# A mixture-of-experts kernel whose last layer norm moves from a pass of its own into the expert loop

## The chip, the cores and the metric

The kernel runs on one core of a Trainium2 chip. The metric is the device time of one execution in microseconds (us), the median of several. The core has five engines that run side by side: TensorE (PE in the profile, with its weight loads as PEld), VectorE (DVE), ScalarE (ACT), GpSimd (POOL) and SyncE (SP), and 16 DMA engines that move data between HBM and the on-chip memory.

## The reference, cut to what matters

```
x  = layernorm(x + attention(x))            # 16 batches x 1024 tokens x 256 values, float32
# mixture of experts: 8 experts, hidden size 1024, two experts per token
logits = x @ wr.T ; vals, idx = top_k(logits, 2) ; gates = softmax of the two
pos  = running count of tokens per expert ; keep = pos < 5120       # a slot beyond 5120 is dropped
h    = gelu(x[slot] @ w1[e] + b1[e]) ; y = (h @ w2[e] + b2[e]) * gate
out  = layernorm(x + sum over the token's kept experts of y)
```

A token has at most two expert entries, in two different experts, and one or both may be dropped.

## The kernel before, in words

T is 16384 tokens, a tile has 128 partitions. The program has three phases, each a block in which the five engines run their own instruction streams and wait for each other by semaphores; between blocks all engines meet.

Phase A goes through the 16 batches, two per loop turn. It computes attention and the first layer norm. All engines' streams are written out by hand in a pipelined order: while TensorE works on batch b, ScalarE and VectorE finish the layer norm and the router of batch b-1. The normalised rows x1 (tile `x1_sb`, two of them, used in turn) are stored by SyncE to two HBM buffers, `x1_rows` and `sum_rows` (`acc_dram`). ScalarE's body is in this order: four copies `kt_out`, parts of the next batch's softmax, `gate_exp`, the copy `g_hi` (L432), `normalize` half 0 (L368), more softmax, `m_hi`, `qt`, `normalize` half 1. TensorE's `maps()` needs `g_lo`, which VectorE makes from `g_hi` (L621). For each token VectorE computes the table slots of its two entries, and GpSimd scatters 16 small DMAs per batch (L323) that write (token, gate) into `slot_table`; entries with no token hold the number of a padding row.

Phase B goes through the experts in order, and within one through blocks of 256 slots, 129 blocks in all. Block n on each engine:

- GpSimd (`body`): waits for the transposes of block n's rows (`xt_ready`), `gather(n+1)`: copies the row numbers (L972) and starts two indirect DMAs that fetch 256 rows of x1 into `rows` (L975); then `put(n)`: two small copies of index and gate (L983, L984), a wait for `y_done`, and two indirect DMAs that add `y` into `sum_rows` in HBM (L988). What `put(n)` writes is the result of the block before n.
- TensorE: `up(0) up(1) up(2) down(0) up(3)`, then `transpose_rows(n+1)` (L1110, waits for `gathered`), `down(1) down(2) down(3)`. Each up and down is 12 matmuls. `down(g)` waits for `h_lo(g)`.
- ScalarE: gelu and the copy `h_hi` (L1031, L1034) for g = 0 to 3, then `split_hi(n+1)` of the transposed rows (L1022).
- VectorE: `h_lo(g)` (L1066) for g = 0 to 3; after g = 1 `scale_y` (L1055), the product of the previous block's result and its gate; after g = 3 `split_lo` (L1047); last `y_raw` = `y_ps` + bias (L1082). In the first two blocks of an expert it also splits the next expert's weights in 8 pieces, one behind each `h_lo` (a cast, L1076, and a subtraction, L1078).
- SyncE loads the weights of expert e+2 when those of e+1 have been split.

Phase C (L1163 on) reads `sum_rows` batch by batch into a ring of four tiles, takes mean and variance on VectorE (L1208, L1211), the reciprocal root on GpSimd (L1223 to L1229, the power at L1225), normalises on ScalarE (L1239), and SyncE stores `out`.

```
def body(n, e, eu):                    # GpSimd, phase B, before
    pool.wait_ge(xt_ready, n + 1)
    gather(n + 1)
    put(n)
```

Of the kernel before, what the change touches and what calls it, by code (L numbers as in the profile page):

```python
# [6 lines left out]
def build(nc, x, x_t, wq, wk, wv_t, wo, wo_t, bo, bo_t, wr_t, w1, b1_t, w2, b2, out):  # L7
# [9 lines left out]
    P = 128  # L17
# [21 lines left out]
    acc_dram = nc.dram_tensor("sum_rows", (T + BLK, D), F, kind="Internal").ap()  # L39
    table_dram = nc.dram_tensor("slot_table", (SLOTS, 2), I, kind="Internal").ap()  # L40
    x1_store = x1_dram[0:T, :].rearrange("(b p t) d -> b p (t d)", p=P, t=TILES)
    acc_store = acc_dram[0:T, :].rearrange("(b p t) d -> b p (t d)", p=P, t=TILES)
# [4 lines left out]
    with outer:  # L47
# [38 lines left out]
        with ExitStack() as phase:  # L86
# [36 lines left out]
            rstd, nshift = sb("rstd", [P, TILES]), sb("nshift", [P, TILES])  # L123
            minus_half = sb("minus_half", [P, TILES])
# [22 lines left out]
            entry = [sb(f"entry{i}", [P, 2, TILES, 2], I) for i in range(2)]  # L147
            blocks_f = sb("blocks_f", [P, 2 * E + 1])
            counts = sb("counts", [P, E])
            pad_entries = sb("pad_entries", [P, TCOLS, 2], I)  # L150
# [44 lines left out]
            entries_written = sems("entries_written", 2)  # L195
            const_step = sem("const_step")
# [17 lines left out]
            def _(sp):  # L214
# [27 lines left out]
                for rows_dram in (x1_dram, acc_dram):  # L242
                    for t in range(BT):
                        sp.dma_start(rows_dram[T + t * P:T + (t + 1) * P, :], zero_rows[:, :]).then_inc(pads_stored, 16)
# [3 lines left out]
                load_xt(3)  # L248

                def body(pair, u, x_left=True, xt_left=True):  # L250
                    b = pair * 2 + u
                    if x_left:
                        sp.wait_ge(r_done, (b + 1) * TILES)
                        load_x(b + 2, u)
                    if xt_left:
# [3 lines left out]
                    for rows in (x1_store, acc_store):  # L259
                        sp.dma_start(rows[b].rearrange("p (t d) -> p t d", d=D), x1_sb[u][:, :, 0:D]).then_inc(x1_stored[u], 16)  # L260

                with sp.Fori(0, NB // 2 - 2) as pair:
                    for u in range(2):
                        body(pair, u)
# [4 lines left out]

                for u in range(2):  # L270
                    sp.wait_ge(x1_stored[u], 32 * (NB // 2))
                sp.wait_ge(pads_stored, 16 * (1 + 2 * BT))
# [3 lines left out]
            def _(pool):  # L276
# [28 lines left out]
                nc.gpsimd.iota(pad_entries[:, :, 0].rearrange("p (a t) -> p a t", t=BT), pattern=[[0, TCOLS // BT], [P, BT]], base=T, channel_multiplier=1).then_inc(pads_made, 1)  # L305
# [12 lines left out]

                def scatter(b, u):
# [8 lines left out]
                pool.wait_ge(pads_stored, 16 * (1 + 2 * BT))  # L328

                def body(pair, u, first, last):  # L330
                    b = pair * 2 + u
                    if not first:
                        norm_chain(b - 1)
                        scatter(b - 1, 1 - u)

                batches(pool, body)
                norm_chain(NB - 1)
                scatter(NB - 1, 1)
# [4 lines left out]
            def _(act):  # L343
# [20 lines left out]
                def normalize(b, u, half):  # L364
# [5 lines left out]
                    if half:  # L370
                        ins.then_inc(x1_done, 1)

# [19 lines left out]
                def body(pair, u, first, last):  # L392
# [60 lines left out]
                batches(act, body)  # L453
                gate_exp(NB - 1)
                for half in range(2):
                    normalize(NB - 1, 1, half)

# [3 lines left out]
            def _(dve):  # L461
# [55 lines left out]
                ROUTE_STEPS = 23  # L517

                def router(b, u, state):
# [37 lines left out]
                    def address(pair, scattered):  # L557
# [6 lines left out]
                                             ALU.arith_shift_right))  # L564
                        if scattered:
                            dve.wait_ge(entries_written[u], 16 * 2 * TILES * pair)
                            V.tensor_scalar(entry[u][:, :, :, 0], entry[u][:, :, :, 0], 2 * N, None, ALU.add)
                        V.scalar_tensor_tensor(where[u][:, :, :], slot_p[:, :, :], float(TCOLS), slot_c[:, :, :], ALU.mult, ALU.add)

                    def gates():  # L570
                        gate = entry[u][:, :, :, 1].bitcast(F)
# [13 lines left out]
                def statistics(b, u):  # L585
                    for t in range(TILES):
                        V.bn_stats(stats[:, t, :], x1_sb[u][:, t, 0:D]).then_inc(stats_done, 1)
                    wait_apart(dve, stats_done, TILES * (b + 1))
# [688 lines left out]
```

## Time and profile before

| | us |
|---|---|
| median of 3 runs | 2361.29 |
| lowest, highest | 2356.31, 2366.18 |
| profiled execution, its own time | 2358.53 |
| its span, first to last instruction | 2356.6 |
| PE busy / ACT / DVE / POOL | 2049.0 / 1136.2 / 1113.5 / 1111.8 |
| mean granted TensorE clock | 0.934 |

The page of the profile has the busy time of each engine, and the same in 40 slices of the span. Slices 14 to 38 of PE are nearly all nines: that is phase B. Before it PE is at 6 to 8 tenths (phase A), and in the last two slices PE does nothing while the DMA rate is highest (phase C). An engine's idle time is put down to the instruction that released it ("<-DVE y L1055"). A POOL span can begin before the engine is free: where a row of POOL starts inside the one before it, the true time is counted from that one's end.

### The profile page before, as it was taken

What the parts mean: (1) busy time and instruction counts of PE and PEld (TensorE: products, weight loads), DVE (VectorE), ACT (ScalarE), POOL (GpSimd) and SP (SyncE); (2) the same over time, 40 slices, a digit from 0 to 9 for tenths busy, and PEclk for the clock granted to TensorE, in tenths of its full rate; (3) what the DMA queues carried; (4) which work ended last, traced back from release to release, by engine and by line L of the source; (5) the groups of instructions that cost most, each with busy time, mean ns of one, the idle gap of its engine ahead of it and who ended that gap; (6) DMA issues with size and microseconds to landing.
All of it is one profiled execution on the core that took longest, in us unless ns stands there. A gap on an engine that the chain in (4) does not pass through costs nothing. (4 is left out here: it accounts for less than half of the span.)

```text
span 2356.6 us, 48196 instructions
## 1 busy us (share of the span) xinstructions
PE 2049.0 (87%) x16208; PEld 1987.8 (84%) x16209; DVE 1113.5 (47%) x2614; ACT 1136.2 (48%) x2516; POOL 1111.8 (47%) x1333
## 2 busy tenths in 40 slices
PE   7887887878744999999999999999999999999910
PEld 6776786777644999999999999999999999999910
DVE  3665565655563435345335333534543534333345
ACT  3444443434332555555555455455455555555547
POOL 0335454453544445444455444544544545444434
PEclk9998898989876999999999999999999999999965
DMA  4323233242223323222322322322322222222258
GB/s 165 108 73 124 90 103 111 72 143 71 68 81 95 80 46 81 45 45 45 79 47 49 76 45 47 80 45 45 80 45 45 45 45 46 46 46 46 46 204 377
DMA packets 130733, 190.10 MB, mean 81 GB/s; under 512 B 19088, under 2 KB 111760, under 8 KB 126480
## 3 DMA queue, kind: packets, MB, share of 16 engines
q0 software_dynamic: 58256, 68.60, 18.1%
q1 hardware_dynamic: 72448, 121.16, 14.8%
q8 instruction: 12, 0.20, 0.0%
q14 instruction: 17, 0.14, 0.0%
HBM read 104.05 MB, written 85.66 MB: 81 GB/s over the span
## 5 line engine op out<-in xcount | busy, mean ns | idle before, releaser
L1031 ACT ACTIVATE h_ps<-h_ps,b_sb 128x256 f32<-128x256 f32 x1032 | 418.5, 444 | 712.6 <-PE h_ps L1129 667.7
L988 POOL DMA_INDIRECT sum_rows<-y,put_idx x260 | 418.9, 1611 | 601.6 <-DVE y L1055 556.3
L1066 DVE TENSOR_TENSOR h_lo<-h_ps,h_hi 128x512 fp32r<-128x512 f32 x516 | 356.6, 691 | 628.7 <-ACT h_hi L1034 600.5
L1145 PE MATMUL y_ps<-w_hi,h_hi 128*128 128x256 f32 x2064 | 586.1, 284 | 0.0
L1129 PE MATMUL h_ps<-bt_hi,w_hi 128*128 128x256 f32 x2064 | 576.1, 279 | 3.2 <-issue 1.7
L1145 PE MATMUL y_ps<-w_hi,h_lo 128*128 128x256 f32 x2064 | 575.8, 279 | 0.0
L1145 PE MATMUL y_ps<-w_lo,h_hi 128*128 128x256 f32 x2064 | 575.1, 279 | 0.0
L1129 PE MATMUL h_ps<-bt_lo,w_hi 128*128 128x256 f32 x2064 | 574.0, 278 | 0.0
L1129 PE MATMUL h_ps<-bt_hi,w_lo 128*128 128x256 f32 x2064 | 574.0, 278 | 0.0
L323 POOL DMA_INDIRECT slot_table<-entry,where x256 | 277.8, 1085 | 304.2 <-DVE entry L575 228.7
L1129 PEld LDWEIGHTS h_ps<-bt_hi,w_hi 128*128 128x128 f32 x2064 | 389.6, 189 | 5.0 <-issue 3.2
L1145 PEld LDWEIGHTS y_ps<-w_hi,h_lo 128*128 128x128 f32 x2064 | 389.6, 189 | 0.0
L1129 PEld LDWEIGHTS h_ps<-bt_lo,w_hi 128*128 128x128 f32 x2064 | 388.7, 188 | 0.0
L1129 PEld LDWEIGHTS h_ps<-bt_hi,w_lo 128*128 128x128 f32 x2064 | 388.6, 188 | 0.0
L1145 PEld LDWEIGHTS y_ps<-w_hi,h_hi 128*128 128x128 f32 x2064 | 388.3, 188 | 0.0
L1145 PEld LDWEIGHTS y_ps<-w_lo,h_hi 128*128 128x128 f32 x2064 | 386.9, 187 | 0.0
L975 POOL DMA_INDIRECT rows<-x_rows,pick_idx x260 | 258.7, 995 | 159.6 <-POOL pick_idx L972 107.5
L1034 ACT ACTIVATE h_hi<-h_ps 128x512 fp32r<-128x512 f32 x516 | 309.0, 599 | 16.4
L788 PE MATMUL g_ps<-kt,x_raw 128*128 128x256 f32 x512 | 144.1, 437 | 85.1 <-issue 64.9
L788 PEld LDWEIGHTS g_ps<-kt,x_raw 128*128 128x128 f32 x512 | 108.9, 221 | 104.7 <-issue 78.7
L1082 DVE TENSOR_TENSOR y_raw<-y_ps,b_sb 128x512 f32<-128x512 f32 x129 | 89.3, 692 | 225.6 <-PE y_ps L1145 222.7
L403 ACT ACTIVATE kt<-t_ps 128x512 f32<-128x512 f32 x64 | 37.9, 598 | 185.4 <-remote 100.5
(191 smaller groups left out, 2843.9 us busy)
## 6 DMA issues: line engine op xcount, KB each, us to landing
xt_raw<-in_x_t SPq DMA_DIRECT2D x16, 1024.0 KB
x_raw<-in_x SPq DMA_DIRECT2D x16, 1024.0 KB
w_raw<-in_w SPq DMA_DIRECT2D x16, 1024.0 KB
x_rows<-x_sb SPq DMA_DIRECT2D x16, 1024.0 KB
sum_rows<-x_sb SPq DMA_DIRECT2D x16, 1024.0 KB
s_in<-sum_rows SPq DMA_DIRECT2D x16, 1024.0 KB, 8.9
out<-s_out SPq DMA_DIRECT2D x16, 1024.0 KB, 6.8
rows<-x_rows,pick_idx POOLq DMA_INDIRECT x260
```

The lines of the kernel that those rows point to most:

```text
L323: pool.indirect_dma_start(out=table_dram, out_offset=bass.IndirectOffsetOnAxis(ap=where[u][:, c, t:t + 1], axis=0), in_=entry[u][:, c, t, ...
L403: nc.scalar.activation(kt[:, j % 2, :], t_ps[:, j % 2, :], ACT.Copy).then_inc(kt_done, 1)
L788: ins = nc.tensor.matmul(g_sum[:, k, :], x_raw[u][:, t, k * P:(k + 1) * P], kt[:, j % 2, i * D:(i + 1) * D], start=(t == 0 and k == 0), st ...
L975: pool.indirect_dma_start(out=rows[:, t, :], out_offset=None, in_=x1_dram, in_offset=bass.IndirectOffsetOnAxis(ap=pick_idx[:, t:t + 1], ax ...
L988: pool.indirect_dma_start(out=acc_dram, out_offset=bass.IndirectOffsetOnAxis(ap=put_idx[:, t:t + 1], axis=0), in_=y[:, t, :], in_offset=No ...
L1031: nc.scalar.activation(half, half, ACT.Gelu_apprx_tanh, bias=b1_sb[:, bass.ds(e * FT + 2 * g + i, 1)]).then_inc(gelu_done, 1)
L1034: nc.scalar.activation(h_hi[:, g, :], h_ps[:, g, :], ACT.Copy).then_inc(h_hi_done, 1)
L1066: V.tensor_tensor(h_lo[:, g, :], h_ps[:, g, :], h_hi[:, g, :].bitcast(F), ALU.subtract).then_inc(h_lo_done, 1)
L1082: V.tensor_tensor(y_raw[:, :, :], y_ps[:, :, :], b2_sb[:, bass.ds(e * D, D)].rearrange("p (a d) -> p a d", a=1).broadcast_to([P, BT, D]), ...
L1129: ins = nc.tensor.matmul(h_ps[:, g, (f % 2) * BLK:(f % 2 + 1) * BLK], w[:, c:c + P], v[:, k, :], start=(i == 0), stop=(i == 3 * DK - 1))
L1145: ins = nc.tensor.matmul(y_ps[:, t, :], v[:, g, h:h + P], w[:, c:c + D], start=(f == 0 and t == 0 and part == 0), stop=(f == FT - 1 and t ...
```

## The change

Phase C and the buffer `sum_rows` are gone. A table entry has four words in place of two: token, place of the sum so far, gate, and a flag. The entry that lies in the higher slot is the token's last one if the other one isn't dropped; its second word is then the token, that of the first entry is out of range. Results go straight to `out` with plain indirect DMAs that skip rows out of range.

In phase B the first entry of a token writes x1 + gate * y, un-normalised, to `out`; the last one fetches that row as its `base`, adds gate * y, and normalises with the flag deciding by arithmetic (factor 1 and mean 0 where it isn't the last). x1 of a block stays on chip: ScalarE copies `rows` to `x1_next`, VectorE copies that to `base`, and `take_up_sums` overwrites by DMA those rows of `base` that have a sum in `out`. A token both of whose entries are dropped gets its result in phase A: ScalarE normalises x1 once more (`renormalize`, 8 activations per batch), and SyncE stores it to `out` where it stored the second copy of x1 before.

An expert has 5 blocks at least, where it had 4. The weights' split is spread over blocks 0, 2 and 3 of an expert. The first block of an expert on GpSimd (`first_body`) puts, waits until it has landed, and only then takes up sums; VectorE adds up late in the block after it (`turn == 1`).

```diff
@@ GpSimd, phase A @@
+                def norm_again(b, u):
+                    if not (isinstance(b, int) and b < 2):
+                        pool.wait_ge(alone_done, b - 1)
+                    nc.gpsimd.tensor_tensor(again[u][:, :], mean_var[:, :, 1], rstd[:, :], ALU.mult).then_inc(again_step, 1)
+                    nc.gpsimd.tensor_tensor(again[u][:, :], again[u][:, :], rstd[:, :], ALU.mult).then_inc(again_step, 1)
+                    nc.gpsimd.tensor_scalar(again[u][:, :], again[u][:, :], EPS, None, ALU.add).then_inc(again_step, 1)
+                    nc.gpsimd.tensor_tensor(again[u][:, :], again[u][:, :], minus_half[:, :], ALU.pow).then_inc(again_done, 1)
...
@@ ScalarE, phase A @@
+                def renormalize(b, u):
+                    act.wait_ge(again_done, b + 1)
+                    act.wait_ge(alone_stored, 16 * b)
+                    for t in range(TILES):
+                        ins = nc.scalar.activation(alone[:, t, :], x1_sb[u][:, t, 0:D], ACT.Copy, scale=again[u][:, t:t + 1])
...
                     if more:
                         q_softmax(b + 1, 1 - u, 1)
+                    if not first and not (isinstance(b, int) and b == 1):
+                        renormalize(b - 2, u)
                     if not first:
                         gate_exp(b - 1)
@@ VectorE, phase A, address() @@
+                        V.tensor_tensor(leads[:, 0, :], slot_i[:, 1, :], slot_i[:, 0, :], ALU.is_ge)
+                        step(V.tensor_tensor(leads[:, 1, :], slot_i[:, 0, :], slot_i[:, 1, :], ALU.is_ge))
...
+                        V.scalar_tensor_tensor(entry[u][:, :, :, 1], leads[:, :, :], DROPPED, entry[u][:, :, :, 0], ALU.mult, ALU.add)
+                        for c in range(2):
+                            V.scalar_tensor_tensor(entry[u][:, c, :, 3].bitcast(F), slot_f[:, 1 - c, :], DROPPED, leads[:, c, :],
+                                                   ALU.is_ge, ALU.is_ge)
@@ GpSimd, phase B @@
+                def root(n):
+                    pool.wait_ge(var_done, n + 1)
+                    G.tensor_tensor(rstd[:, :], rstd[:, :], minus_half[:, :], ALU.pow).then_inc(root_done, 1)
+
+                def take_up_sums(n):
+                    pool.wait_ge(base_done, n + 1)
+                    G.tensor_copy(base_idx[:, :], column(n + 1, 1)).then_inc(base_ready, 1)
+                    wait_apart(pool, base_ready, n + 1)
+                    for t in range(BT):
+                        pool.indirect_dma_start(
+                            out=base[:, t, :], out_offset=None, in_=out_dram,
+                            in_offset=bass.IndirectOffsetOnAxis(ap=base_idx[:, t:t + 1], axis=0),
+                            bounds_check=T - 1, oob_is_err=False).then_inc(base_loaded, 16)
+
+                def scalars(n):
+                    G.tensor_copy(put_gate[:, :], column(n, 2).bitcast(F))
+                    G.tensor_copy(put_last[:, :], column(n, 3).bitcast(F)).then_inc(last_ready, 1)
+                    wait_apart(pool, last_ready, n + 1)
+                    G.tensor_scalar(put_part[:, :], put_last[:, :], -1.0, 1.0, ALU.mult, ALU.add).then_inc(put_ready, 1)
+
+                def put(n, more=True):
+                    pool.wait_ge(put_done, 16 * BT * n + 16)
+                    G.tensor_copy(put_idx[:, :], column(n, 0)).then_inc(put_idx_ready, 1)
+                    pool.wait_ge(y_done, n + 1)
+                    if more:
+                        scalars(n + 1)
+                    wait_apart(pool, put_idx_ready, n + 1)
                     for t in range(BT):
                         pool.indirect_dma_start(
-                            out=acc_dram, ..., in_=y[:, t, :], in_offset=None, compute_op=ALU.add).then_inc(added, 16)
+                            out=out_dram, ..., in_=y[:, t, :], in_offset=None,
+                            bounds_check=T - 1, oob_is_err=False).then_inc(put_done, 16)
...
+                def first_body(n, e, eu):
+                    pool.wait_ge(next_done, n + 1)
+                    gather(n + 1)
+                    root(n)
+                    put(n)
+                    pool.wait_ge(put_done, 16 * BT * (n + 1) + 16)
+                    take_up_sums(n)
+
                 def body(n, e, eu):
-                    pool.wait_ge(xt_ready, n + 1)
+                    pool.wait_ge(next_done, n + 1)
                     gather(n + 1)
+                    take_up_sums(n)
+                    root(n)
                     put(n)
@@ ScalarE, phase B, behind split_hi(n + 1) @@
+                def keep_rows(n):
+                    act.wait_ge(base_done, n)
+                    act.wait_ge(gathered, 16 * BT * (n + 1))
+                    nc.scalar.activation(x1_next[:, :, :], rows[:, :, :], ACT.Copy).then_inc(next_done, 1)
@@ VectorE, phase B @@
+                def add_up(n):        # waits y_raw_done, put_ready, base_loaded
+                    for t in range(BT):
+                        ins = V.scalar_tensor_tensor(y_raw[:, t, :], y_raw[:, t, :], put_gate[:, t:t + 1], base[:, t, :],
+                                                     ALU.mult, ALU.add)
+                def next_base(n):     # waits next_done
+                    V.tensor_copy(base[:, :, :], x1_next[:, :, :]).then_inc(base_done, 1)
+                def spread(n):        # bn_stats and bn_aggr of 2 tiles, then
+                    V.tensor_scalar(rstd[:, :], mean_var[:, :, 1], EPS, None, ALU.add).then_inc(var_done, 1)
+                    V.tensor_tensor(mean[:, :], mean_var[:, :, 0], put_last[:, :], ALU.mult).then_inc(sum_step, 1)
+                def factors(n):
+                    dve.wait_ge(root_done, n + 1)
+                    V.tensor_tensor(rstd[:, :], rstd[:, :], put_last[:, :], ALU.mult).then_inc(sum_step, 1)
+                    V.tensor_tensor(rstd[:, :], rstd[:, :], put_part[:, :], ALU.add).then_inc(sum_step, 1)
+                def finish_rows(n):   # waits put_done
+                    for t in range(BT):
+                        ins = V.tensor_scalar(y[:, t, :], y_raw[:, t, :], mean[:, t:t + 1], rstd[:, t:t + 1], ALU.subtract, ALU.mult)
+
+                    late = turn == 1
+                    if not late:
+                        add_up(n)
+                        next_base(n)
                     for g in range(UNITS):
                         h_lo(g)
-                        if g == 1:
-                            scale_y(n)
+                        if late and g == 1:
+                            add_up(n)
+                            next_base(n)
+                        if g == (2 if late else 0):
+                            spread(n)
+                        if g == (3 if late else 1):
+                            factors(n)
+                            finish_rows(n)
                         if g == UNITS - 1:
                             split_lo(n + 1)
-        (all of phase C)
```

## Rows read from the trace of the kernel before

**Rows 1.** Busy time by stage: us, busy (count) of each engine, clock, DMA share.

```profile
740.00:2250.00 1510.00, 1496.81 (x12901) 1493.92 (x12900) 650.42 (x1147) 773.85 (x1678) 744.42 (x907) 1.00 0.30 53
2262.00:2356.60 94.60, 0.00 (x0) 0.00 (x0) 53.31 (x256) 64.29 (x128) 37.84 (x65) 0.50 0.86 355
```

**Rows 2.** Costliest groups of the page: count, busy us, mean ns, idle before.

```profile
L988 POOL DMA_INDIRECT sum_rows<-y,put_idx x260 | 418.9, 1611 | 601.6 <-DVE y L1055 556.3
L1082 DVE TENSOR_TENSOR y_raw<-y_ps,b_sb 128x512 f32<-128x512 f32 x129 | 89.3, 692 | 225.6 <-PE y_ps L1145 222.7
```

**Rows 3.** POOL in order of time, one block of phase B: start us, us.

```profile
1534.21 1.61 POOL L988 DMA_INDIRECT sum_rows<-y,put_idx  x1 [4.79 <-DVE y L1055]
1536.13 1.58 POOL L988 DMA_INDIRECT sum_rows<-y,put_idx  x1 [0.30 <-issue]
1537.14 0.77 POOL L972 COPY pick_idx<-table 128x2 int32 x1
1538.78 1.01 POOL L975 DMA_INDIRECT rows<-x_rows,pick_idx  x1 [0.87 <-POOL pick_idx L972]
1540.09 0.98 POOL L975 DMA_INDIRECT rows<-x_rows,pick_idx  x1 [0.30 <-DMA sum_rows<-y,put_idx]
...
1541.21 0.18 POOL L984 COPY put_gate<-table 128x2 f32 x1
```

**Rows 4.** DVE in order of time over the same block.

```profile
1530.76 0.69 DVE L1066 TENSOR_TENSOR h_lo<-h_ps,h_hi 128x512 fp32r<-128x512 f32 x1 [2.20 <-ACT h_hi L1034]
...
1532.73 0.61 DVE L1055 TENSOR_SCALAR y<-y_raw,put_gate 128x256 f32<-128x256 f32 x2
...
1539.47 0.69 DVE L1082 TENSOR_TENSOR y_raw<-y_ps,b_sb 128x512 f32<-128x512 f32 x1 [1.87 <-PE y_ps L1145]
...
1551.00 0.69 DVE L1082 TENSOR_TENSOR y_raw<-y_ps,b_sb 128x512 f32<-128x512 f32 x1 [1.74 <-PE y_ps L1145]
```

**Rows 5.** PE in order of time, transposes: at an expert's start, and inside an expert.

```profile
1522.95 0.66 PE L1110 MATMUL tb_ps<-ident,rows 128*128 128x128 f32 x4 [0.73 <-DMA rows<-x_rows,pick_idx]
...
1534.47 0.60 PE L1110 MATMUL tb_ps<-ident,rows 128*128 128x128 f32 x4
```

**Rows 6.** POOL in order of time, end of phase B and phase C.

```profile
2248.61 0.18 POOL L983 COPY put_idx<-table 128x2 int32 x1 [2.52 <-DMA sum_rows<-y,put_idx]
...
2271.82 1.67 POOL L1225 TENSOR_TENSOR rstd_c<-rstd_c,minus_half_c 128x8 f32<-128x8 f32 x1
...
2273.97 0.25 POOL L1229 TENSOR_SCALAR nshift_c<-nshift_c 128x8 f32<-128x8 f32 x1 [0.19 <-POOL nshift_c L1227]
```

**Rows 7.** DVE in order of time, the last block of phase B.

```profile
2247.79 0.69 DVE L1082 TENSOR_TENSOR y_raw<-y_ps,b_sb 128x512 f32<-128x512 f32 x1 [1.87 <-PE y_ps L1145]
```

**Rows 8.** Groups by line, phase C.

```profile
L1208 DVE BATCH_NORM_STATS2 stats_c<-s_in 128x6 f32<-128x256 f32 x128 | 43.3, 411 | 40.0 <-DMA s_in<-sum_rows 40.0
```

**Rows 9.** Groups by line, 1000 to 2200 us.

```profile
L1076 DVE CAST w_hi<-w_raw 128x512 fp32r<-128x512 f32 x40 | 19.5, 487 | 0.0
```

**Rows 10.** DVE in order of time, phase A.

```profile
502.28 0.17 DVE L562 TENSOR_SCALAR slot_p<-slot_i 128x16 int32<-128x16 int32 x1
...
504.89 0.48 DVE L633 SCALAR_TENSOR_TENSOR m_raw<-o_ps,rzk,bo_sb 128x264 f32<-128x264 f32 x1
...
510.68 2.28 DVE L480 TENSOR_TENSOR w_lo<-xt_raw,w_hi 128x2048 fp32r<-128x2048 f32 x1
```

**Rows 11.** ACT in order of time, phase A.

```profile
497.87 0.21 ACT L375 ACTIVATE gap_exp<-gap 128x8 f32<-128x8 f32 x1 [0.67 <-DVE gap L546]
499.07 0.60 ACT L432 ACTIVATE g_hi<-g_ps 128x512 fp32r<-128x512 f32 x1 [1.00 <-PE g_ps L788]
499.57 2.07 ACT L368 ACTIVATE x_sb<-x_sb,nshift,rstd 128x256 f32<-128x256 f32 x4
```

**Rows 12.** POOL in order of time, phase A.

```profile
510.71 3.09 POOL L323 DMA_INDIRECT slot_table<-entry,where  x1 [0.30 <-issue]
```

**Rows 13.** PE in order of time, phase A, first matmul of `maps()`.

```profile
502.73 0.28 PE L710 MATMUL g_ps<-wvo_hi,g_hi 128*128 128x264 f32 x1
```

More of the change, by code:

```diff
@@ L123, in build @@
             rstd, nshift = sb("rstd", [P, TILES]), sb("nshift", [P, TILES])
+            again = [sb(f"again{i}", [P, TILES]) for i in range(2)]
+            alone = sb("alone", [P, TILES, D])
             minus_half = sb("minus_half", [P, TILES])
@@ L254, in body @@
                         load_x(b + 2, u)
+                    if not (isinstance(pair, int) and pair == 0 and u == 0):
+                        store_alone(b - 1)
                     if xt_left:
@@ L258, in body @@
                     sp.wait_ge(x1_done, b + 1)
-                    for rows in (x1_store, acc_store):
-                        sp.dma_start(rows[b].rearrange("p (t d) -> p t d", d=D), x1_sb[u][:, :, 0:D]).then_inc(x1_stored[u], 16)
-                with sp.Fori(0, NB // 2 - 2) as pair:
+                    sp.dma_start(x1_store[b].rearrange("p (t d) -> p t d", d=D), x1_sb[u][:, :, 0:D]).then_inc(x1_stored[u], 16)
+                for u in range(2):
+                    body(0, u)
+                with sp.Fori(1, NB // 2 - 2) as pair:
                     for u in range(2):
@@ L304, in _ @@
                 made(nc.gpsimd.memset(pad_entries[:, :, :], 0))
-                nc.gpsimd.iota(pad_entries[:, :, 0].rearrange("p (a t) -> p a t", t=BT), pattern=[[0, TCOLS // BT], [P, BT]], base=T, channel_multiplier=1).then_inc(pads_made, 1)
+                for w in range(2):
+                    made(nc.gpsimd.iota(pad_entries[:, :, w].rearrange("p (a t) -> p a t", t=BT), pattern=[[0, TCOLS // BT], [P, BT]], base=T, channel_multiplier=1))
+                nc.gpsimd.memset(leads[:, :, :], 0).then_inc(pads_made, 1)
                 def norm_chain(b):
@@ L942, in experts @@
                         blocks, before = blocks_of(eng, half * 2 + eu)
-                        with eng.Fori(0, blocks) as block:
+                        if first_body is not None:
+                            first_body(before, half * 2 + eu, eu)
+                        with eng.Fori(0 if first_body is None else 1, blocks) as block:
                             body(before + block, half * 2 + eu, eu)
@@ L1009, in body @@
                     put(n)
-                experts(pool, body)
+                experts(pool, body, first_body=first_body)
                 total = all_blocks(pool)
-                put(total)
-                pool.wait_ge(added, 16 * BT * (total + 1) + 16)
+                root(total)
+                put(total, False)
+                pool.wait_ge(put_done, 16 * BT * (total + 1) + 16)
                 pool.wait_ge(gathered, 16 * BT * (total + 1))
@@ L1088, in expert @@
                     blocks, before = blocks_of(dve, e)
-                    for turn in range(2):
-                        body(before + turn, e, eu, None if last else turn)
-                    with dve.Fori(2, blocks) as block:
+                    for turn in range(4):
+                        body(before + turn, e, eu, turn, not last)
+                    with dve.Fori(4, blocks) as block:
                         body(before + block, e, eu)
```

234 lines of the change are left out of this document (107 added, 127 removed).

## Prediction, made before the changed kernel ran

> **What bounds the kernel now.** I read the stages first, then the order of time inside one block of phase B on each engine, then the end of the kernel and one batch of phase A. In phase B PE is busy 1496.8 of 1510 us at a granted clock of 1.00, the full 2.4 GHz [rows 1]: TensorE bounds 64% of the kernel. One block takes 11.55 us there (the 11.53 between two `y_raw` starts in [rows 4]; neighbours have 11.59), and there are 129 [rows 2]. Every other engine has idle time that costs nothing: POOL waited 556 us in all for `y` before its puts, 4.3 us per block [rows 2]. Phase C is another kind of stage: PE does nothing and the DMA engines are 86% busy [rows 1]. So the change takes away a stage that moves data and puts its arithmetic beside a stage that PE fills. The question is whether it stays beside it.
>
> **Removed: phase C.** The last `y_raw` ends at 2247.79 + 0.69 = 2248.5 [rows 7], the span at 2356.6: 108.1 us come after it. The new tail behind that `y_raw`: two additions 0.9, statistics and variance 1.3, the power 0.6, factors and final rows 1.05 (prices below), 0.87 before an indirect DMA, two puts 2.3, 2.5 for the landing (a wait of POOL for a put lasted 2.52 behind its issue [rows 6]), and 0.5 to close: 10. Saved: 98 us. This is sure; the reads and adds in HBM in phase B that go with it save nothing, since no row has PE waiting for them.
>
> **Phase B, POOL's round.** In the new order POOL's work per block is a closed ring: `y_done` -> scalars -> puts -> gather(n+1) -> sums(n) -> root(n) -> VectorE's factors and final rows -> `y_done`. POOL can't begin root(n) before both transfers are issued, and VectorE can't finish `y` before root. So a block can't be shorter than the sum, however early rows are ready:
> - scalars: two copies 0.31 (from 1541.07 to 1541.39), 0.04 to start, then a self-wait 0.19 and a small operation 0.25 [rows 3, 6]. An indirect DMA behind a wait starts 0.87 late, after a copy as after `y` (1533.34 to 1534.21) [rows 3, 4]; that lies partly beside the small operation. 1.2 to 1.7, I take 1.45.
> - puts: before, 1.61 + 0.30 + 1.58. Those accumulate; the plain gather takes 1.01 + 0.30 + 0.98 = 2.29 [rows 3]. I take 2.29, since the new put is plain; the bound above is 3.49.
> - gather: copy 0.19, 0.87, 2.29: 3.35 [rows 3]. Sums: the same kinds of instruction, 3.35.
> - root: the power over 128x8 takes 1.67, a small operation 0.25 [rows 6]. If it goes by element, 2 columns of 8 take 0.25 + 1.42 / 4 = 0.6; bounds 0.25 and 1.67. I take 0.6.
> - VectorE: two dependent small operations of 0.2 (0.17 each [rows 10] and the gap), two products 0.61 [rows 4], 0.04 to start: 1.05.
>
> Sum 12.1 us against 11.55. POOL's idle 4.3 is used up: it gave 1.2 back by the plain puts, and took 3.35 + 0.6 + 0.9 + the turn-around through VectorE. Bounds: 11.5 with every lower end, 14.6 with every upper one.
>
> VectorE itself fits: it had 2.20 idle before `h_lo(0)` [rows 4], and two additions of 0.48 [rows 10] and a copy of about 0.42 to 0.49 [rows 9] go there; statistics are 0.41 per tile [rows 8]. ScalarE's extra copy, 0.6, is hidden by its idle time. But while VectorE waits for root in `factors` at g = 1, `h_lo(2)` stands behind it, and `down(2)` on PE behind that. Count from the start of `h_lo(0)`: transposes at 3.70 (1534.47 - 1530.77 [rows 4, 5]), `down(1)` at 4.1, and 1.4 per down (12 of 96 matmuls) gives 5.5 for `down(2)`. The new `y_done` is naturally at 3.9, `h_lo(2)` 0.65 later, so PE has 0.9 of slack once, and from then on each block takes 12.1. An expert has 16 blocks on average; in blocks 4 to 15: 12 x 0.55 - 0.9 = 5.7 us; 8 experts: 46 us.
>
> **Phase B, the start of an expert.** In block 0 root comes early, `y_done` at 3.8. Then puts issued at 3.8 + 3.74 = 7.5, landed (2.5) at 10.05, sums issued 13.4, and only then gather for block 2, issued 16.75, landed 19.25. PE wants these rows at 11.55 + 3.70 = 15.25: it stalls 4.0. Rows landed sooner would make this 3.3. Block 1: base landed at 15.9, additions and copy to 17.2, sums to 20.55, root 21.15, `y_done` 22.2. One ring later, at 34.3, comes the `y_done` of block 2; a weight piece stands behind it (a cast 0.49 [rows 9] and a subtraction as long as `h_lo`, together 1.2 us), then `h_lo(2)`, which ends at 36.15. PE, whose block began its count at 23.1 + 4.0 = 27.1, wants it at 32.6: 3.5, and 0.4 more for `h_lo(3)`. Block 3 is free again (sums are issued before its statistics). Pieces in block 0: 0.6. Together 8.5 per expert. Today's stalls there go off: phase B is 1510 us for 129 blocks, 19 more than 129 x 11.56 [rows 1, 2], 2.3 per expert, of which the wait for rows beside the weights' load, 0.73 [rows 5], stays; 1.5 goes. 7 x 8 = 56 us. Phase B: +102.
>
> **Phase A.** `renormalize` is 8 activations, as long as the four that take 2.07 [rows 11]: 4.0 us at ScalarE, put before `g_hi`. It had 0.67 idle before `gap_exp` and 1.00 before `g_hi` at 499.07 [rows 11]; `g_hi` now begins 4.0 - 1.7 = 2.3 later, at 501.4. Behind it: `g_lo`, `maps()` on PE, which began at 502.73 [rows 13] and so keeps its place to within 0.2; but VectorE's slot arithmetic comes after `g_lo` and is 0.5 longer (five small operations at 0.1 and one step more at 0.2), so the next maximum, `m_raw`, `m_hi` and `m_lo` come 1.5 later, and `attend(0)` with them. 14 batches x 1.5: +22 us; bounds 0 (the delay is caught up in the 4 us of idle between batches) and 50. `norm_again` on POOL (2.7 us per batch) is hidden by its 16 us of waiting for the router; the store to `out` replaces another of the same size, and stands in SyncE's queue between loads whose own waits end later, so nothing waits for it. Set-up on POOL and the minimum of 5 blocks: nothing, no expert has fewer.
>
> **Sum.** 2358.5 (the profiled execution's own time) - 98 + 102 + 22 = 2384.5. The median is 2.8 above the profiled execution, so 2387.
>
> **A rule weighed.** A scatter of POOL took 3.09 us, not the 1.0 of a gather [rows 3], when VectorE began a 2.28 us operation with two operands in on-chip memory 0.03 before it [rows 10, 12]. Base additions and copy are such operations, and fall beside the gather's second DMA. The Trainium skill ("SBUF — State Buffer", on the shared port pair) says that the pair is an exclusive lock held for the whole instruction, taken by a float32 copy, which enters a 2-port mode, and for reads by an operation with two inputs there. The trace agrees for two inputs, 2.28 beside 3.09. By that rule the ring grows by up to the copy's 0.42, which is the fourth case below.
>
> **Cases.**
> - Forecast, 0.42: ring of 11.9 to 12.5; 2360 to 2420. A third of it lies under 2375.
> - Ring within 11.55, 0.30. All lower ends: the 0.87 hides, power 0.25. PE stays the bound in plain blocks, the starts of experts cost 5 x 8 = 40, phase A 5: 2358.5 - 98 + 45 = 2305 (to 2345 with ring 11.7). For it: the two waits of 0.87 before gather and sums are idle time, not work. Against it: they are in every block. This is the other side; it decides at a ring of 11.7.
> - The put or the power stays at its upper price, 0.08: ring 13.2, 12 x 1.65 - 0.9 = 19 per expert, 9 at the start: 224, 2358.5 - 98 + 224 + 22 = 2507. Against it: the plain gather at 0.98.
> - VectorE and POOL block each other, 0.13: ring 12.5, 40 us more: 2424.
> - Phase A costs the 50: 0.07, 2412.
>
> That the change doesn't do what it says is not among them: phase C can't be left in. The range is 2315 to 2450, which leaves about 0.1 below and 0.1 above; the forecast's own is 2360 to 2420. A measurement here tells 0.5%, 12 us, from no change: faster 0.26 (the second case but its top), same 0.18 (a third of the first and that top), slower 0.56.
>
> **What would show it.** In the new trace, groups of POOL by line: puts at 1.0 rather than 1.6, the power 0.6. `y_raw` start to start: 12.1 in blocks 4 to 15; POOL's longest wait no longer `y` but under 1.2 per block; VectorE idle before the first factor product "<-POOL rstd" about 0.6; PE idle 0.5 per block before an L1145 matmul, and in each expert one stall of 3 to 4 us before L1110 "<-DMA rows". Phase A: `maps()` at the same distance from the batch's start, `attend(0)` 1.5 later. The forecast is wrong if PE stays over 98% busy in phase B.

## The result: slower by 5.2%, 95 us above the forecast

The changed kernel takes 2482.03 us (median of 4, 2480.21 to 2486.15), the kernel before 2360.71 beside it: ratio 1.0515, 95% interval 1.0493 to 1.0537. The profiled execution took 2480.21, its span 2478.5. I had 2387, range 2315 to 2450: right in sign, outside in size. By stage, from the `y_raw` starts of the two traces (profiled executions, us):

| | before | after | change | forecast |
|---|---|---|---|---|
| start to first `y_raw` | 755.8 | 760.6 | +4.8 | +22 |
| first to last `y_raw` (phase B) | 1492.0 | 1706.6 | +214.6 | +102 |
| of it: 97 blocks from the fifth of an expert on | 11.56 each | 13.03 each (median 12.84) | +143 | +46 |
| of it: first four blocks of 8 experts | | | +72 | +56 |
| behind the last `y_raw` start | 108.8 | 11.2 | -97.5 | -98 |

The stage row, where [rows 1] had PE busy 1496.81 of 1510 us:

```profile
740.00:2470.00 1730.00, 1598.38 (x12904) 1568.85 (x12904) 1025.05 (x2568) 855.87 (x1808) 1036.45 (x1685) 0.98 0.17 56
```

There are as many matmuls as before (12904, before 12901), but PE is idle for 132 us of this stretch, where it was for 13, and the granted clock is 0.98 in the mean. The groups of the page after (answering to [rows 2]): the puts fell from 1611 to 1045 ns, and PE now has 96 us of idle time ahead of the second layer:

```profile
L1083 POOL DMA_INDIRECT out<-y,put_idx x260 | 271.8, 1045 | 130.1 <-issue 128.1
L1048 POOL DMA_INDIRECT rows<-x_rows,pick_idx x260 | 266.1, 1023 | 156.1 <-issue 113.7
L1062 POOL DMA_INDIRECT base<-out,base_idx x258 | 263.9, 1023 | 159.7 <-issue 82.0
L1317 PE MATMUL y_ps<-w_hi,h_hi 128*128 128x256 f32 x2064 | 615.3, 298 | 96.4 <-DVE h_lo L1227 96.0
```

POOL after in order of time, one plain block, from the first put to the next (answers to [rows 3]); between two rows stands idle time, in brackets with its releaser:

```profile
1117.26 1.10 POOL L1083 DMA_INDIRECT out<-y,put_idx  x1 [0.69 <-issue]
1118.67 0.99 POOL L1083 DMA_INDIRECT out<-y,put_idx  x1 [0.31 <-issue]
1119.64 0.22 POOL L1045 COPY pick_idx<-table 128x2 int32 x1
1120.74 1.09 POOL L1048 DMA_INDIRECT rows<-x_rows,pick_idx  x1 [0.88 <-issue]
1122.13 0.97 POOL L1048 DMA_INDIRECT rows<-x_rows,pick_idx  x1 [0.30 <-DVE base L1185]
1123.10 0.20 POOL L1059 COPY base_idx<-table 128x2 int32 x1
1124.18 1.04 POOL L1062 DMA_INDIRECT base<-out,base_idx  x1 [0.88 <-issue]
1125.53 1.00 POOL L1062 DMA_INDIRECT base<-out,base_idx  x1 [0.31 <-issue]
1126.56 0.74 POOL L1054 TENSOR_TENSOR rstd_b<-rstd_b,minus_half_b 128x2 f32<-128x2 f32 x1
1127.26 0.18 POOL L1077 COPY put_idx<-table 128x2 int32 x1
1128.72 0.18 POOL L1069 COPY put_gate<-table 128x2 f32 x1 [1.28 <-DVE y L1211]
...
1130.10 1.10 POOL L1083 DMA_INDIRECT out<-y,put_idx  x1 [0.69 <-issue]
```

From put to put 12.84 us, and POOL's only long wait for another engine is the 1.28 for `y`. VectorE after, over the same block (answers to [rows 4]), shows why that wait is no slack: VectorE itself waited 2.09 for the power, and gave `y` back 1.25 behind it. The ring is closed.

```profile
1114.97 0.74 DVE L1211 TENSOR_SCALAR y<-y_raw,mean_b,rstd_b 128x256 f32<-128x256 f32 x2
...
1121.39 0.69 DVE L1185 COPY base<-x_next 128x512 f32<-128x512 f32 x1
...
1127.33 0.16 DVE L1203 TENSOR_TENSOR rstd_b<-rstd_b,put_last 128x2 f32<-128x2 f32 x1 [2.09 <-POOL rstd_b L1054]
1127.52 0.16 DVE L1205 TENSOR_TENSOR rstd_b<-rstd_b,put_part 128x2 f32<-128x2 f32 x1
1127.81 0.74 DVE L1211 TENSOR_SCALAR y<-y_raw,mean_b,rstd_b 128x256 f32<-128x256 f32 x2
1128.46 1.28 DVE L1227 TENSOR_TENSOR h_lo<-h_ps,h_hi 128x512 fp32r<-128x512 f32 x2
```

The end after, DVE in order of time (answers to [rows 7]); the span ends 11.2 behind the start of this row:

```profile
2467.21 0.69 DVE L1250 TENSOR_TENSOR y_raw<-y_ps,b_sb 128x512 f32<-128x512 f32 x1 [3.64 <-PE y_ps L1317]
```

### The profile page after: what moved, and what is told of

It is laid out like the page before. It is cut to its first block, busy times and chain, and to the rows that moved or that the text cites. A ratio compares the mean times of both kernels' runs of the same rounds, so it can differ in the third digit from the quotient of the medians.

```text
span 2478.5 us, 52379 instructions
## 1 busy us (share of the span) xinstructions
PE 2146.0 (87%) x16208; PEld 2059.5 (83%) x16209; DVE 1444.7 (58%) x3868; ACT 1199.0 (48%) x2646; POOL 1404.7 (57%) x2114
## 4 chain that ended last, share of the span: by engine, by line
POOL 19%; issue 17%; PE 16%; DVE 14%; DMA 2%; POOLq 2%; DVEq 1%; ACT 0%; ACTq 0%
PE y_ps L1317 14%; POOL base L1062 7%; POOL rows L1048 5%; POOL rstd_b L1054 4%; DVE y_raw L1250 2%; DVE base L1185 2%; DVE h_lo L1227 2%; DVE y L1211 2%; PE h_ps L1301 2%; DVE y_raw L1178 2%; POOL out L1083 1%; DMA rows<-x_rows,pick_idx 1%; POOL base_idx L1059 1%; DVE rstd_b L1205 1%; DVE rstd_b L1203 1%
## 5 line engine op out<-in xcount | busy, mean ns | idle before, releaser
L1317 PE MATMUL y_ps<-w_hi,h_hi 128*128 128x256 f32 x2064 | 615.3, 298 | 96.4 <-DVE h_lo L1227 96.0
L1317 PE MATMUL y_ps<-w_lo,h_hi 128*128 128x256 f32 x2064 | 592.1, 287 | 0.0
L1317 PE MATMUL y_ps<-w_hi,h_lo 128*128 128x256 f32 x2064 | 591.7, 287 | 0.0
L1301 PE MATMUL h_ps<-bt_lo,w_hi 128*128 128x256 f32 x2064 | 584.7, 283 | 0.0
L1317 PEld LDWEIGHTS y_ps<-w_hi,h_hi 128*128 128x128 f32 x2064 | 401.8, 195 | 119.2 <-DVE h_lo L1227 118.7
L1227 DVE TENSOR_TENSOR h_lo<-h_ps,h_hi 128x512 fp32r<-128x512 f32 x516 | 346.0, 685 | 98.5 <-ACT h_hi L1151 87.8
L1317 PEld LDWEIGHTS y_ps<-w_hi,h_lo 128*128 128x128 f32 x2064 | 402.2, 195 | 0.0
L1317 PEld LDWEIGHTS y_ps<-w_lo,h_hi 128*128 128x128 f32 x2064 | 401.9, 195 | 0.0
L1062 POOL DMA_INDIRECT base<-out,base_idx x258 | 263.9, 1023 | 159.7 <-issue 82.0
L1083 POOL DMA_INDIRECT out<-y,put_idx x260 | 271.8, 1045 | 130.1 <-issue 128.1
```

The lines of the kernel that those rows point to most:

```text
L1062: pool.indirect_dma_start(out=base[:, t, :], out_offset=None, in_=out_dram, in_offset=bass.IndirectOffsetOnAxis(ap=base_idx[:, t:t + 1], a ...
L1083: pool.indirect_dma_start(out=out_dram, out_offset=bass.IndirectOffsetOnAxis(ap=put_idx[:, t:t + 1], axis=0), in_=y[:, t, :], in_offset=No ...
L1227: V.tensor_tensor(h_lo[:, g, :], h_ps[:, g, :], h_hi[:, g, :].bitcast(F), ALU.subtract).then_inc(h_lo_done, 1)
L1301: ins = nc.tensor.matmul(h_ps[:, g, (f % 2) * BLK:(f % 2 + 1) * BLK], w[:, c:c + P], v[:, k, :], start=(i == 0), stop=(i == 3 * DK - 1))
L1317: ins = nc.tensor.matmul(y_ps[:, t, :], v[:, g, h:h + P], w[:, c:c + D], start=(f == 0 and t == 0 and part == 0), stop=(f == FT - 1 and t ...
```

## The experiments

Theory 1: POOL's closed ring sets each plain block. Rivals: the landing of puts at an expert's start, VectorE and POOL lengthening each other, PE or VectorE by themselves, phase A. "After" is the changed kernel, "before" the one before it. Runs of one group shared a chip and the runs of the kernel before on it; ratios are against those. "Plain block" is the median distance of two `y_raw` starts from an expert's fifth block on: 11.55 us before, 12.84 after. Before: 2362.83 in the first group.

**Root first.** `root(n)` ahead of `take_up_sums(n)` in the loop body:

```
-    take_up_sums(n)
     root(n)
+    take_up_sums(n)
```

> One edit to the changed kernel: in GpSimd's plain body of phase B root(n) stands before take_up_sums(n) and not behind it; no engine does more or less. Theory 1 (the closed round y_done - scalars - puts - gather - sums - root - VectorE - y_done sets the block, 12.84 us in the trace of after): VectorE's 1.27 us and the 0.17 behind it then run beside the sums, POOL's own work is left, 11.4 to 11.8 us; PE needs 11.56. Plain blocks 11.6 to 11.8, starts of experts unchanged, time about 2370 (2355 to 2390). Rival A (VectorE has too much work: 3.5 us more per block, and h_lo queues behind it) and rival B (the DMA engines or the shared memory ports slow everything): the work is the same, so 12.8 per block and 2482 stay.

2373.2 us, ratio 1.0048 (1.0025 to 1.0071). One swap of two calls takes the ratio from 1.0515 to 1.0048, some 110 of the 121 us. Plain block 11.94. By the traces phase B is 115 us shorter: 81 in the plain blocks, and 34 in the first four blocks of the experts, where none was expected. The ring theory holds for the plain blocks; but PE had next to no idle time in them (0.08 us per block) and yet took 11.94, not 11.55, which no theory had. That led to the place runs below.

**Early index.** The copies of the gather's and the sums' indices a block earlier:

```
 def put(n):
     copy put_idx
+    copy pick_idx for gather(n + 2)
     wait y_done, scalars(n + 1)
+    copy base_idx for sums(n + 1)
```

> The changed kernel with its order, but the copies of the gather's and the sums' row numbers are made one block earlier, beside GpSimd's wait for y, into the same tiles (a tile of its own for the first block of an expert), so that the indirect DMAs don't start 0.88 behind a copy of 0.2. Theory 1: the round loses about 2 x (0.2 + 0.88 - 0.3) = 1.55 and gets back about 0.2: 11.5, so PE's 11.56 sets plain blocks again; time 2340 (2325 to 2365). If the 0.88 is work of GpSimd that only moves: 12.4 to 12.8 and 2440 or more. Rivals A and B: no change.

2411.4, ratio 1.0211 (1.0187 to 1.0235): half of the gain that I had expected. Plain block 12.39. POOL got to the power earlier, but VectorE, in order of time in this kernel, couldn't use it yet: `h_lo(1)` stands ahead of the factors in its program, and ScalarE gave the input of `h_lo(1)` only at 1108.11:

```profile
1108.11 0.69 DVE L1242 TENSOR_TENSOR h_lo<-h_ps,h_hi 128x512 fp32r<-128x512 f32 x1 [1.64 <-ACT h_hi L1166]
1108.72 0.15 DVE L1218 TENSOR_TENSOR rstd_b<-rstd_b,put_last 128x2 f32<-128x2 f32 x1
```

The power had ended at 1107.67. So the ring got a new member, ScalarE's `h_hi(1)`. (The tiles that this edit adds also moved the matmuls' operands; their pace was 0.116 us here, see the place runs. PE had idle time in these blocks, 0.43 us each, so it isn't what set them.)

**First sums free.** In an expert's first block the sums come from `x1_rows`, without the wait for landed puts (the sums are then not the right ones):

```
-    pool.wait_ge(put_done, 16 * BT * (n + 1) + 16)
-    take_up_sums(n)
+    take_up_sums(n, x1_dram)
```

> The changed kernel, but in the first block of an expert the sums are fetched from x1_rows and not from out, and the wait for the landed put before it is gone (the values of those rows are another's; the DMA is of the same size and skips the same rows). Theory 1 for the starts (put, its landing, sums and only then the gather for block 2 stand in one row on GpSimd): the wait of 2 to 2.5 us goes, block 2 of an expert falls from 17.2 to about 15, 8 x 2 to 3 us: time 2460 (2452 to 2468). If the starts are set by VectorE's late order and its weight pieces instead: unchanged within 4 us.

2480.4, ratio 1.0506 (1.0480 to 1.0532): no gain that can be told. In the mean over the experts, block 1 fell from 13.72 to 12.41 us, and block 2 rose from 17.23 to 18.04, block 3 from 12.32 to 12.61. Most of what the wait had cost, PE then waited later.

**More on POOL, before.** The kernel before with one more copy and one more pair of gathers per block:

```
     gather(n + 1)
+    copy more_idx; two indirect gathers into more_rows
     put(n)
```

> The kernel before with one more copy of row numbers and one more pair of indirect DMAs per block on GpSimd (256 rows of x1 into a tile that nothing reads), put between gather and put. It adds 3.4 us to POOL per block and as many bytes as a full take-up of sums, but no turn-around. Theory 1: POOL had 4.3 us of idle per block, 0.9 stays, PE stays the bound: within 0.5% of before (2361), at most 2375 where POOL's rare pauses of 2 us now show. Rival B (DMA engines or ports): 5% slower, as the changed kernel is.

2423.3, ratio 1.0268 (1.0240 to 1.0295): a miss. POOL in order of time in this run:

```profile
1412.51 0.18 POOL L994 COPY put_gate<-table 128x2 f32 x1
1414.31 1.62 POOL L998 DMA_INDIRECT sum_rows<-y,put_idx  x1 [1.61 <-DVE y L1069]
...
1424.55 0.17 POOL L994 COPY put_gate<-table 128x2 f32 x1
1426.33 1.62 POOL L998 DMA_INDIRECT sum_rows<-y,put_idx  x1 [1.61 <-DVE y L1069]
```

The old kernel has such a ring too: VectorE's `y` waits for `put_gate`, copied behind the gathers, and POOL for `y`. The 1.61 are 0.62 of VectorE and 0.87 in front of an indirect DMA, not slack. The ring here is 12.02 from put to put; without the 3.2 added it is 8.8, so the slack before was 11.55 - 8.8 = 2.7 us, not the 4.3 that the wait showed. From put to put it takes 11.98 to 12.08 in 103 of 128 blocks and more in the others (12.7 where an expert starts), 1555 us in all, where phase B is 1553: the ring set this kernel's phase B. The plain block, 11.89 by the median, is shorter because PE, behind after an expert's start, then makes up for it. The edit also moved the matmuls' operands by 32 bytes, and their pace from 0.116 to 0.118 us; no put came later by that.

**Place of the tiles.** An unused tile stands ahead of `rows`; its size moves `rows` and every tile allocated behind it. Second group (before 2358.37): the changed kernel, and root-first, with a larger one, and the kernel before without it.

```
 after, root first:  - sb("spare", [P, 16])   + sb("spare", [P, 32])
 before:             - sb("spare", [P, 16])
```

> The changed kernel with 64 bytes more of unused tile ahead of rows, nothing else. In the kernel before, rows, bt_hi, bt_lo, h_hi and h_lo begin 64 bytes above a multiple of 128 in each partition; the new small tiles moved them to a multiple of 128, and matmuls now start 0.119 us apart where they started 0.1156 us apart, at the same granted clock. Two theories. Place: the distance is set by where those tiles lie; here it goes back to 0.1156, but a plain block stays at 12.84, since there POOL's ring and not PE sets it; only the starts of experts gain, about 10 us: 2470 (2462 to 2480). Traffic: the distance is set by what POOL, VectorE and the DMAs do beside PE; here it stays 0.119 and the time 2482.

2487.3, ratio 1.0559 (1.0518 to 1.0600). Matmuls are 0.116 apart again, plain block 12.80: POOL's ring sets it, and PE only waits longer (for `h_lo` 121 us in phase B, where it was 96). The 10 us at the starts didn't come.

> The kernel before without its unused tile spare of 64 bytes, so that rows, bt_hi, bt_lo, h_hi and h_lo begin at a multiple of 128 bytes. Place: matmuls 0.119 apart instead of 0.1156, and as PE bounds each block here, a block takes 11.9 instead of 11.55: 129 x 0.34 = 44 us more, 2405 (2395 to 2412). Traffic: no change, 2361.

2396.7, ratio 1.0171 (1.0134 to 1.0209): +38, in the range expected. Plain block 11.85. Busy time by window, 30 us in the middle of an expert, first the kernel before, then this one; both are all busy at a clock of 1.00, with 262 and with 254 matmul records (a few records can be missing from a trace; the pace below is from the distances of neighbours, not from these counts):

```profile
1550.00:1580.00 30.00, 30.00 (x262) 30.00 (x261) 12.04 (x22) 16.09 (x35) 13.67 (x18) 1.00 0.27 48
```

```profile
1550.00:1580.00 30.00, 30.00 (x254) 30.00 (x253) 12.36 (x22) 15.68 (x34) 14.77 (x17) 1.00 0.26 39
```

> The changed kernel with root(n) before the sums' gather, and with the 64 bytes more ahead of rows. With root first alone PE had no idle time in plain blocks and a block took 11.93 with matmuls 0.119 apart. Place: the matmuls go back to 0.1156 and a block to 11.6: 2373 - 129 x 0.33 = 2330 (2318 to 2340; POOL's own round is 11.6 there and may hold a few us back). Traffic: 2373 as without the pad.

2357.1, ratio 0.9989 (0.9967 to 1.0010), 0.6% under root-first by the ratios, as against the 1.8% I had expected. The same window in root-first and in this one:

```profile
1480.00:1510.00 30.00, 30.00 (x253) 30.00 (x253) 17.73 (x44) 15.58 (x33) 19.89 (x35) 1.00 0.16 51
```

```profile
1480.00:1510.00 30.00, 30.00 (x261) 29.69 (x260) 19.62 (x53) 17.03 (x37) 20.65 (x33) 1.00 0.19 59
```

That place sets the pace is shown in three kernels, each changed by the pad alone; which tile's place it is, is not. Plain block 11.71; some of the rest went into longer waits of PE for rows (52.5 us in phase B, 41.7 in root-first).

**Root first and early index together** (here, too, the tiles are 64 bytes above a multiple of 128):

> Root first and, besides, the copies of the gather's and the sums' indices made a block earlier, so that no indirect DMA stands 0.88 behind its copy; here too rows begins 64 bytes above a multiple of 128. Ring theory: POOL's round shrinks by 2 x 0.58 and root's 0.75 no longer stands behind the sums, so it is about 10.5 and PE bounds the plain blocks at 11.6; the starts of experts cost about 2.5 us each more than before: first y_raw 760 + 128 x 11.6 + 20 + 11 = 2276 to 2300, say 2287. Rival (what is left is not the ring but VectorE's work before h_lo(2)): a block stays at 12 or more, 2335 or more.

2348.7, ratio 0.9952 (0.9923 to 0.9982), where 2287 was expected. Plain block 11.55, as before: POOL's ring is out of the way. But first to last `y_raw` is 1562, where it was 1492 before. Busy time by window, inside an expert: a stretch at full pace, the stall in the fifth block, and what came behind it.

```profile
1570.00:1580.00 10.00, 10.00 (x89) 10.00 (x88) 8.29 (x21) 4.76 (x12) 6.57 (x12) 1.00 0.21 60
1577.50:1586.30 8.80, 6.92 (x60) 6.62 (x58) 6.28 (x18) 5.65 (x12) 6.54 (x8) 1.00 0.87 307
1586.40:1590.80 4.40, 4.40 (x25) 4.40 (x26) 1.08 (x2) 1.12 (x2) 2.51 (x7) 0.61 0.14 43
```

PE in order of time in this run:

```profile
1586.40 0.66 PE L1297 MATMUL tb_ps<-ident,rows 128*128 128x128 f32 x4 [1.98 <-issue]
```

The gather was issued beside the load of weights (DMA engines 87% busy) and landed late; PE stood 1.98 us, and then ran through 25 records in 4.4 us where 39 belong by the first window, at a granted clock of 0.61: the stall was paid for twice. PE's waits over phase B (us in all, times, longest) name what it stood for:

```profile
PE tb_ps L1297 <- DMA rows<-x_rows,pick_idx: 41.9, 23, 2.8
```

**Rows ahead.** Third group; its chip grants PE the full clock in phase A, and the kernel before takes 2213.52 there. Besides the two edits above, rows are gathered two blocks ahead:

```
 first block: root, puts, + gather(n + 2), wait for landed puts, sums
 others:      root, sums, copies, + gather(n + 2), puts
```

> Root first and early index copies, and besides the rows are gathered two blocks ahead: gather(n+2) stands ahead of the puts of block n (in an expert's first block: behind its puts, in the time in which they land). In root-first-early PE stalled 2 to 3 us for rows in block 2 and 2.1 us in block 4 of an expert, each time beside the load of weights, and matmuls ran 0.21 us apart (granted clock about half) for about 15 to 19 matmuls after such a stall. Theory (stalls for rows, each with its slow stretch behind it): they go, and the starts cost what they cost before: first y_raw 755 + 1492 + 10 to 25 + 11 = 2280 (2265 to 2305). Rival (what holds the starts is VectorE's work between h_lo(1) and h_lo(2) or the landing of the sums): 2325 or more.

2176.6, ratio 0.9836 (0.9823 to 0.9849): 1.6% faster than the kernel before, and by the ratio faster than root first and early index without it. Phase B took 1531 us, not the 1502 to 1517 expected; half of the hoped-for 3.4%. PE's waits for rows are all but gone, one for VectorE stays:

```profile
PE y_ps L1338 <- DVE h_lo L1248: 28.3, 19, 2.5
...
PE tb_ps L1303 <- DMA rows<-x_rows,pick_idx: 1.5, 5, 0.5
```

It is in an expert's block 2 (about 2.0 us in seven of eight), where VectorE waits for a power that stands behind the gather and puts of the late block 1; and in block 4 (1.3 in six of eight) and block 0 (2.4 in two), which no run took apart.

**No power.** A product in its place (normalised values wrong): `ALU.pow` becomes `ALU.mult`.

> The changed kernel with a product in place of the power in root(n) (the normalised values are then wrong). Ring: POOL's round loses 0.75 - 0.25 = 0.5 us, each of 97 plain blocks 0.5 and each expert's first blocks about 1: 48 + 8 = 56 less, 2425 (2415 to 2435). If PE or VectorE sets the block: within 5 of 2482.

2270.0, ratio 1.0247 (1.0232 to 1.0263); the changed kernel measured 1.0572 on another chip that grants the full clock in phase A (fourth group), so 70 us less by the medians and 66 by phase B (1637 against 1703), where 56 was expected; block 12.29. The product took 0.21 where the power took 0.74:

```profile
1107.28 0.21 POOL L1054 TENSOR_TENSOR rstd_b<-rstd_b,minus_half_b 128x2 f32<-128x2 f32 x1
```

**Short copy.** `next_base` copies 8 of 256 columns (sums wrong):

> The changed kernel with next_base copying 8 of 256 columns (the sums are then wrong). In the changed kernel that copy takes 0.69 beside an indirect DMA of 1.10; with root first, where no indirect DMA runs beside it, it takes 0.43, and the same DMA 0.99. Theory: the two lengthen each other, and the ring is 0.1 shorter without the long copy: 97 x 0.1 = 10 less, 2472 (2465 to 2480). The fourth case of the forecast, 0.4 per block by a lock: 40 less, 2442.

2331.6, ratio 1.0532 (1.0516 to 1.0549). Phase B 1698 against 1703. The gather beside the copy took 1.00 instead of 1.09; block 12.83. The 40 us of the forecast's fourth case are excluded.

**Phase A.** Fourth group (before 2214.73): `renormalize` with one activation for eight, and both kernels again for their profiles.

> The changed kernel with one activation over all eight tiles in renormalize in place of eight (every tile takes the first one's factor, so the stored rows are wrong); ScalarE then spends about 2.2 us there in place of 4.0. The forecast let ScalarE put each batch off by 1.5 us; by it a batch is 1.5 shorter: 14 x 1.5 = 21 less than after. The two traces at a granted clock of 0.86 in phase A (15 batches in 617.2 us after, 614.7 before) let at most 2.5 us go; where the clock stays at 1.00 in phase A and a batch takes 32.1, PE leaves ScalarE less time, and it could be up to 12. I take 3 at the lower clock, 10 at the full one.

2339.6, ratio 1.0563 (1.0545 to 1.0581).

> The changed kernel unchanged, beside the others on the same chip: ratio 1.05, plain blocks 12.84, whatever the clock of phase A.

2340.1, ratio 1.0572 (1.0554 to 1.0589).

> The kernel before unchanged, for its profile on this chip: phase B 1492 from first to last y_raw as ever; its phase A tells how much of it was the clock: 15 batches in 615 us at a granted clock of 0.86, about 470 at 1.00, where the changed kernel takes 480.

2218.0 in its single run. ScalarE's group in the first two, 100 to 500 us: 2.0 us per batch with one activation, 3.3 with eight (26.2 and 42.9 in 13 batches).

```profile
L409 ACT ACTIVATE alone<-x_sb,again 128x2048 f32<-128x2048 f32 x13 | 26.2, 2017 | 0.0
```

```profile
L410 ACT ACTIVATE alone<-x_sb,again 128x256 f32<-128x256 f32 x104 | 42.9, 512 | 0.0
```

First `y_raw` is at 622.1 in both, where I had expected up to 10 us less: ScalarE's time there sets nothing. In the kernel before it is at 610.3; a batch takes 31.5 there and 32.1 after. So phase A costs 12 at the full clock (9 in the batches, 3 behind them) and 5 at the lower one (2.5 in the batches). What takes the 0.6 per batch, these runs don't say.

## Why the prediction was wrong, by its own steps

The profiled execution took 2480.21 where the sum gave 2384.5: 97 us more in the plain blocks and 16 at the experts' starts, less 17 in phase A, which by luck hid a part of it.

- **What bounds, and that it moves to POOL's ring:** right. The waits it named came: VectorE for the power, PE ahead of the y matmuls ("0.5 per block" was 0.75: 96 us in 129), PE not over 98% busy in phase B. But VectorE stood 2.09 for the power where 0.6 was forecast, and `y` stayed POOL's longest wait, 1.28 per block.
- **Phase C removed, -98:** right, -97.5.
- **The step that failed: the ring's sum, 12.1.** Forecast and measured (1115.71, where `y` ended, to 1128.55): scalars and lead 1.45, 1.55; puts 2.29, 2.40; gather 3.35, 3.44; sums 3.35, 3.43; power 0.6, 0.77; VectorE 1.05, 1.25. Together 12.84. Every term came out above its forecast, by 2 to 28%, and only what is above 11.55 counts: 6% on the ring made 0.55 into 1.29. Where the terms differ: the old rows had 0.98 to 1.01 for an indirect DMA, and the first of a pair takes 1.04 to 1.10 here; two columns of the power took 0.74, not a base and a quarter of the rest (0.6); and a subtraction and product by two scalars takes 0.41 where the product took 0.34. Of the 97 us missed in the plain blocks, 72 are this (97 x 0.74), 18 are in the next point, and 7 are the slack of 0.9 per expert that I took off. No power (66 less for 0.53 of ring) and root first (81 less in the plain blocks) show that this ring set the plain blocks.
- **Not in it: pauses.** The mean of plain blocks is 0.19 over the median, 18 us; 15 of these are in the six blocks with a pause and the ones right behind. About once in 114 indirect DMAs POOL stands 2.1 us between two of a pair in place of 0.30. After issues six indirect DMAs a block where before issued four, so the pauses come more often, and in a ring without slack:

```profile
1233.98 1.04 POOL L1062 DMA_INDIRECT base<-out,base_idx  x1 [0.88 <-POOL base_idx L1059]
1237.19 1.00 POOL L1062 DMA_INDIRECT base<-out,base_idx  x1 [2.17 <-issue]
```

- **Start of an expert, +56:** +72. Its places were right (rows in block 1, `h_lo(2)` in block 2, 3.3 us longest), its sizes not. In the mean over the experts block 0 grew by 1.7 us (forecast 0.6), block 1 by 2.2 (PE's wait for rows was 1.3, not 4.0), block 2 by 4.6 (2.7 for `h_lo`, near the forecast's 3.9), block 3 by 0.8 (nothing forecast). A part is the slow stretch behind a stall (14 in phase B, some 220 matmuls 0.21 apart). And the stalls of the kernel before, taken off, were 1.6 us per expert, not 2.3: the 1510 us that I took for phase B is the length of the window in [rows 1], and by its `y_raw` starts phase B is 1492. That the landing of puts was behind it was wrong: first-sums-free moved the wait on, no more.
- **Phase A, +22:** +5, and wrong in mechanism: taking 1.3 us per batch off ScalarE's eight activations gained nothing, so they put nothing off.
- **The rivals:** "ring within 11.55", a third of my chance, was what a sum with every lower end gave; no row had ended that low. "VectorE and POOL block each other" had 0.4 per block; 0.1 at most is there. The upper price, ring 13.2 and 2507, had 0.08, and was the nearest of all in time, by luck: its condition, a put or power at the upper price, didn't come (puts 1.05 in the mean, power 0.74). My range left it out.
- **What no part of it held:** that small new tiles move the big ones. It cost nothing in after (the ring hid it); without the ring it costs: 38 us in the kernel before, 0.6%, some 14 us, in root-first.

## What to carry to other kernels

When two engines wait for each other once per block, add up the whole ring, with the turn-around, and compare it with the block: what is above it comes back in every block, and an error in the sum comes back whole. A sum that lies within a few per cent of the block, as 12.1 against 11.55, can't tell the excess to within a factor of two. Put what the other engine waits for first in the queue (here the power ahead of the sums: 110 us for a swap of two lines). After adding any small tile, look whether the operands of the matmuls still start where they did.

## What the runs showed of the hardware that I had not expected

- With `rows`, `bt_hi`, `bt_lo`, `h_hi` and `h_lo` 64 bytes above a multiple of 128 bytes in each partition, matmuls of 128x256 start 0.116 us apart in the mean; at a multiple of 128, 0.119; in the one kernel with 96 above it (more POOL; all of these but `rows`), 0.118. The granted clock is 1.00 in each. Why is open, and which of the tiles matters.
- Behind a longer stall of PE, as the 1.98 us above, mostly 11 to 17 matmuls run 0.21 apart instead of 0.12 (0.61 of the clock granted over 4.4 us): a stretch at the lower of the two levels, 1.2 GHz. The changed kernel has 14 such stretches in phase B, some 20 us in all, each within 2 us behind a stall of 1.96 to 3.29; the kernel before has none in its first profile and two in the one of the fourth group, behind stalls of 1.99 and 1.89.
- About every 110 to 115 indirect DMAs of POOL, 2.1 us between two in place of 0.30, six times in the changed kernel's phase B. In the kernel before, whose puts accumulate, it is 0.86, three times, each between two gathers. Why is open.
- On two chips PE was granted a clock of 1.00 in phase A where the others gave 0.88, and phase A took 610 us instead of 756; phase B, 1497 and 1492, didn't care. Busy time by window, 100 to 500 us, the kernel before on the one and on the other:

```profile
100.00:500.00 400.00, 393.49 (x2600) 358.53 (x2600) 310.06 (x922) 224.65 (x559) 252.98 (x254) 1.00 0.42 131
```

```profile
100.00:500.00 400.00, 321.56 (x1931) 286.89 (x1929) 230.28 (x688) 172.56 (x416) 189.45 (x193) 0.88 0.33 103
```

PE was 80% busy at 0.88 and 98% at 1.00. What makes a chip the one or the other is open.
